# Feed-forward up products as three float32r products of split slots and split weights

## What is computed

```python
def ff(w1e, w2e, w3e):
    h = jax.nn.gelu(xf @ w2e * (xf @ w1e), approximate=False)
    return h @ w3e
y_all = jax.vmap(ff)(w1, w2, w3)      # w1, w2: (8, 128, 256), w3: (8, 256, 128)
y = y_all[m, jnp.arange(n)]           # each token takes the output of one expert
```

## Time and profile before

| | us |
|---|---|
| median of 3 runs | 568.18 |
| lowest, highest run | 567.49, 568.57 |
| span of the profiled execution (8050 instructions) | 554.8 |
| PE busy | 475.4 (86%) |
| DVE busy | 368.3 (66%) |
| ACT busy | 230.6 (42%) |
| POOL busy | 160.9 (29%) |
| up products in the chain that ended last | 4% of the span |

### The profile page before, as it was taken

The page is one execution under the profiler, slowest core; times in us unless marked ns, Lnnn a source line. Parts: engine busy times, 40 slices in busy tenths (PEclk is TensorE's granted clock), DMA queues, the critical chain, the costliest instruction groups (busy, mean ns, idle before and its releaser), DMA issues.

```text
span 554.8 us, 8050 instructions
## 1 busy us (share of the span) xinstructions
PE 475.4 (86%) x2788; PEld 263.0 (47%) x2788; DVE 368.3 (66%) x1023; ACT 230.6 (42%) x418; POOL 160.9 (29%) x200
## 2 busy tenths in 40 slices
PE   3877877899999999998999899999979889888940
PEld 2434344454454545544563555355444536555630
DVE  3635888766767676677658675857883645765685
ACT  1262531643463355426432842364144142445432
POOL 4311222401313241224302430313233465052432
PEclk9989998999999999999999999999998899899985
DMA  7500000000030003000300030011043052023224
GB/s 208 175 2 2 2 1 2 1 1 2 2 79 2 0 4 79 1 2 4 77 2 2 3 77 2 2 47 33 1 155 76 25 159 100 2 63 95 63 67 99
DMA packets 19093, 23.82 MB, mean 43 GB/s; under 512 B 2630, under 2 KB 15374, under 8 KB 18158
## 3 DMA queue, kind: packets, MB, share of 16 engines
q1 hardware_dynamic: 15308, 18.19, 12.0%
q0 software_dynamic: 1648, 4.07, 2.7%
q10 hardware_dynamic: 2098, 1.05, 0.7%
HBM read 16.71 MB, written 6.28 MB: 41 GB/s over the span
## 4 chain that ended last, share of the span: by engine, by line
PE 69%; DVE 13%; ACT 9%; issue 4%; POOL 2%; DMA 1%; ACTq 1%; POOLq 0%; DVEq 0%
PE ps_r L990 8%; PE ps_r L1017 7%; PE ps_st L955 6%; PE ps_r L860 5%; PE ps_r L709 5%; PE ps_st L1235 4%; ACT pt L1895 4%; PE ps_st L944 4%; PE ps_r L1006 3%; PE ps_r L763 3%; PE ps_r L837 3%; DVE rmax_a L1333 2%; PE ps_st L744 2%; PE ps_st L747 2%; PE ps_r L969 2%
## 5 line engine op out<-in xcount | busy, mean ns | idle before, releaser
L600 POOL TENSOR_TENSOR qkr<-qkr,prod 128x512 f32<-128x512 f32 (+1 forms) x48 | 52.3, 1096 | 191.3 <-DVE prod L1459 190.3
L1333 DVE TENSOR_REDUCE rmax_a<-ps_r 128x2 f32<-128x512 f32 (+1 forms) x96 | 61.2, 686 | 32.5 <-PE ps_r L837 32.3
L1895 ACT ACTIVATE pt<-ps_st 128x1024 f32<-128x1024 f32 x48 | 46.6, 1025 | 61.3 <-PE ps_st L747 61.3
L1333 DVE TENSOR_REDUCE rmax<-ps_r 128x2 f32<-128x512 f32 (+1 forms) x96 | 60.7, 683 | 15.3 <-PE ps_r L969 15.0
L709 PE MATMUL ps_r<-cbt 128*128 128x256 bf16 (+1 forms) x192 | 62.0, 323 | 2.6 <-ACT qbuf L1932 1.0
L1904 ACT ACTIVATE pt<-ps_st 128x1024 f32<-128x1024 f32 x48 | 47.2, 1022 | 32.4 <-PE ps_st L955 32.4
L637 POOL TENSOR_TENSOR oT<-pvb,oT 128x1024 f32<-128x1024 f32 x14 | 32.8, 2369 | 78.9 <-DMA oT<-inv_dram 78.9
L990 PE MATMUL ps_r<-pt,vb 128*64 128x512 f32 x192 | 48.2, 607 | 4.5 <-ACT pt L1904 2.7
L1017 PE MATMUL ps_r<-wqkv,xT_b 128*128 128x512 f32 x96 | 45.6, 612 | 4.1 <-DVE rmax_a L1333 3.5
L709 PEld LDWEIGHTS ps_r<-cbt 128*128 128x128 bf16 x192 | 18.6, 97 | 46.5 <-issue 34.2
L955 PE MATMUL ps_st<-qbuf,kbuf 64*128 64x512 f32 x288 | 39.8, 408 | 0.0
(11 more groups left out here) (238 smaller groups left out, 883.2 us busy)
## 6 DMA issues: line engine op xcount, KB each, us to landing
oT<-inv_dram SPq DMA_DIRECT2D x14, 512.0 KB, 5.5
xs_dram<-pvb SPq DMA_DIRECT2D x1, 2048.0 KB
pt<-in_L_ffn_w SPq DMA_DIRECT2D x2, 1024.0 KB, 7.7
ys_dram<-qkr SPq DMA_DIRECT2D x14, 128.0 KB, 1.8
qkr<-xs_dram POOLq DMA_DIRECT2D x4, 256.0 KB, 4.1
x_all<-in_L_attn_x ACTq DMA_DIRECT2D x1, 896.0 KB, 6.2
pvb<-xs_dram POOLq DMA_DIRECT2D x3, 256.0 KB, 4.8
out<-x_all SPq DMA_DIRECT2D x1, 640.0 KB, 3.9
```

What stands on the lines that cost most here:

```text
L600: nc.gpsimd.tensor_tensor(part, part, prod[:, (3 * t + i) % 2, 0:w], ALU.add).then_inc(add_in, 1)
L1333: nc.vector.tensor_reduce(heads_of(i), ps_r[:, b, :].rearrange("p (h k) -> p h k", h=4 if i < 4 else 2), AX.X, ALU.max).then_inc(free[b], 1)
L1895: nc.scalar.activation(pt_a(kind)[:, 8 * half:8 * half + 8, :], ps_st[:, c % 2, :, :].rearrange("p b (h t) -> p (b h) t", h=4), ACT.Exp, s ...
```

## The change

Each fp32 up product becomes three float32r products that add up in PSUM: high slots times high weights, high slots times low weights, low slots times high weights. A high part is the value as a float32r tile holds it, written by an ACT copy; a low part is the value less its high part, by a DVE subtraction.

- Weights: in the last attention step ACT makes the high parts in four copies of 1024 elements a row (`high_weights`) into `qbuf[0]`, and DVE the low parts in four subtractions (`low_weights`) into `qbuf[1]`, which holds the queries of sequence 7 until their scores are done.
- Slots: `take_slots` writes the high part into `kbuf[0]`, and DVE's new `low_slots(n)` the low part, from the same PSUM bank. DVE now frees the bank; ACT tells of the high part by `xg_hi_in`.
- `up(n)` waits for `xg_hi_in`, issues the products with high slots of all its tiles, waits for `emptied(xg{n})`, and issues the products with low slots.

```diff
+        whi, wlo = (b[:, :] for b in qbuf)
...
-        xgT = [xT_a, xT_b]
+        xg_hi, xg_lo = (kbuf[0][:, 2 * T * i:2 * T * (i + 1)].rearrange("p (a t) -> p a t", a=2) for i in range(2))
...
+        whi_in, wlo_in, xg_hi_in = sem("whi_in"), sem("wlo_in"), sem("xg_hi_in")
...
             def up(n, i, g):
 
-                emptied(pe, NB, f"xg{n}")
+                pe.wait_ge(xg_hi_in, n + 1)
                 if n > 1:
                     pe.wait_ge(prod_e, n - 1)
                 for t, tile in enumerate(g):
-                    mm = nc.tensor.matmul(ps_st[:, n % 2, t, :], xgT[n % 2][:, P * t:P * (t + 1)],
-                                          w12_flat[:, bass.ds(expert[tile] * 2, 2 * HID)], start=True, stop=True)
+                    rows, at = xg_hi[:, n % 2, P * t:P * (t + 1)], bass.ds(expert[tile] * 2, 2 * HID)
+                    nc.tensor.matmul(ps_st[:, n % 2, t, :], rows, whi[:, at], start=True, stop=False)
+                    nc.tensor.matmul(ps_st[:, n % 2, t, :], rows, wlo[:, at], start=False, stop=False)
+                emptied(pe, NB, f"xg{n}")
+                for t, tile in enumerate(g):
+                    mm = nc.tensor.matmul(ps_st[:, n % 2, t, :], xg_lo[:, n % 2, P * t:P * (t + 1)],
+                                          whi[:, bass.ds(expert[tile] * 2, 2 * HID)], start=False, stop=True)
                 mm.then_inc(up_full, 1)
...
-            pe.wait_ge(w12_in, 32)
+            pe.wait_ge(whi_in, 4)
+            pe.wait_ge(wlo_in, 4)
...
                 if s == NB - 1:
+                    low_weights(s, 0)
+                    low_weights(s, 1)
+                    low_slots(0, GROUPS[0][1])
...
+            def low_weights(s, i):
+
+                dve.wait_ge(whi_in, 4)
+                dve.wait_ge(sc_b, E_B * s + (4, E_B)[i])
+                for k in range(2):
+                    to, hi = (x.rearrange("p (e w n) -> p e w n", e=E, w=2)[:, E // 2 * k:E // 2 * (k + 1), i]
+                              for x in (wlo, whi))
+                    TT(to, w12[:, E // 2 * k:E // 2 * (k + 1), i], hi.bitcast(F32), ALU.subtract).then_inc(wlo_in, 1)
+
+            def low_slots(n, g):
+
+                b, w = filled(dve, NB, f"xg{n}"), len(g) * P
+                dve.wait_ge(xg_hi_in, n + 1)
+                TT(xg_lo[:, n % 2, 0:w], ps_r[:, b, 0:w], xg_hi[:, n % 2, 0:w].bitcast(F32), ALU.subtract) \
+                    .then_inc(free[b], 1)
...
                     take_hidden(n - 1, GROUPS[n - 1][1])
+                if n + 1 < NG:
+                    low_slots(n + 1, GROUPS[n + 1][1])
                 if n > 1:
                     take_outputs(n - 2, GROUPS[n - 2][1])
...
+                    high_weights(0, 3)
                 take_weights(s, 0)
                 exp(s, 2)
                 exp(s, 3)
+                if s == NB - 1:
+                    high_weights(3, 4)
...
-                nc.scalar.activation(xgT[n % 2][:, 0:w], ps_r[:, b, 0:w], ACT.Copy).then_inc(free[b], 1)
+                nc.scalar.activation(xg_hi[:, n % 2, 0:w], ps_r[:, b, 0:w], ACT.Copy).then_inc(xg_hi_in, 1)
+
+            def high_weights(lo, hi):
+
+                act.wait_ge(w12_in, 32)
+                for k in range(lo, hi):
+                    cols = slice(2 * E * HID // 4 * k, 2 * E * HID // 4 * (k + 1))
+                    nc.scalar.activation(whi[:, cols], w12_flat[:, cols], ACT.Copy).then_inc(whi_in, 1)
```

## The result

The changed kernel took 576.27 us (median of 4 runs, 573.88 to 579.98), the kernel before beside it 568.38: ratio 1.013 (1.009 to 1.017), 7.9 us slower. Two later comparisons gave 1.016 (1.013 to 1.018) and 1.015 (1.013 to 1.017). The sign was as forecast, the size was not: 3.25 us were forecast, 8 to 9 came. The ratios leave out executions over 1.5% above the fastest of the same kernel and are not the quotients of the two medians, from which they differ by up to 0.3%.

The account below looks back on a forecast made before the run. PE was taken to bound the kernel, 69% of its chain of waits. Terms 1.55 + 3.6 - 2.0 - 0.25 + 0.35 gave +3.25 us on 568.18: 571.4 us, range 568.4 to 574.0.

Parts of the forecast that it names:

- groups 5, 9, 11, 13: Odd feed-forward groups: the table read waits for the low slots, 0.9 us for each of four, +3.6 us.
- groups 0 to 3 (start of up(4)): First feed-forward groups: low_slots(3) stands behind slots(1) on DVE, so up(4) starts at 492.05 instead of 490.51, +1.55 us.
- even groups 4, 6, 10, 12, 14: Feed-forward groups without a table read, low slots ready early: shorter products gain 0.40 us each, -2.0 us.
- groups 7 and 8: Feed-forward loop: ACT's two table loads cover PE's delay and group 8's gain; up(7) ends earlier, -0.25 us for both.
- group 15 to the end: Last, one-tile group: low part ready 0.9 us after its start, so it and the tail end 0.35 us later.
- preparation: Last attention step: ACT's four copies and DVE's four subtractions of weights fit idle time, cost 0.
- The held table read: Odd groups: PE's table read, behind the low products' open wait, starts about 0.95 us after the first product.
- The rule of the Trainium skill: PE's sequencer fetches on past an open wait; rival that the table read is not held: 566.7 us, 12%.
- TensorE falls to 1.2 GHz: Rival, group 3: its new wait drops the clock for 3.4 us, +0.6 to +1.5 us, 572.0 to 572.9; 18%.
- The 13.4 us outside the span: Whole kernel: the time between the 554.8 us profiled span and the 568.18 us median, taken as unchanged.
- The bound of 1.6 us: Preparation: were DVE's last two weight subtractions twice as slow, invert_weights would start up to 1.6 us late.
- My own sign of being wrong: Listed sign against the forecast: the last attention step takes longer than now; no size given.

Follow-up runs that it names:

- after_again: The changed kernel again, unchanged, for a closer time and a second profile, on the quick chip: 565.02 us beside 555.51 for the kernel before, ratio 1.016.
- fp32_late_free: The kernel before with fp32 products, plus the changed kernel's waits for an unused DVE difference ahead of the table read: 563.57 us beside 555.51, ratio 1.012.
- read_early: The changed kernel with the table read issued between the high products and the wait for the low slots: 578.61 us beside 569.07, ratio 1.018.
- before_again: The kernel before, unchanged, run again for a second profile: 569.25 us beside 569.07, ratio 1.000.
- low3_early: The changed kernel with low_slots(3) moved ahead of slots(1) on DVE: 574.31 us beside 568.78 for the kernel before, ratio 1.010.
- low_first_unchecked: The changed kernel with low_first's order and the table read's bounds check skipped: 568.51 us beside 568.78 for the kernel before, ratio 1.000.
- low_first_unchecked_2: The kernel of low_first_unchecked run again, on the quick chip: 555.85 us, ratio 0.997 to the kernel before.
- low_first: The changed kernel with every low_slots(n + 1) ahead of take_hidden(n - 1) on DVE: 572.72 us beside 568.78 for the kernel before, ratio 1.007.
- unchecked_after: The changed kernel with the bounds check of the table read's values skipped: 560.04 us, ratio 1.007 to the kernel before.

## Why the prediction came out as it did
Forecast and measured terms, the latter as changed (after_again) less before in the table of periods (the loop's terms and the end add up to +6.6):

| term | forecast | measured |
|---|---|---|
| groups 5, 9, 11, 13 | +3.6 | +3.63 |
| groups 0 to 3 (start of up(4)) | +1.55 | +2.49 (group 3 +3.04, groups 0 to 2 -0.55) |
| even groups 4, 6, 10, 12, 14 | -2.0 | -0.35 |
| groups 7 and 8 | -0.25 | +0.47 |
| group 15 to the end | +0.35 | +0.36 |
| preparation | 0, at most 1.6 | 0 on slow chips, 1.6 to 4.8 on the quick one |

- **The held table read** was right to 0.2 us: it starts 1.03 us behind the first product (forecast 0.95) in groups 5, 7 and 9, 1.06 to 1.13 in 11 and 13 (once, in group 5 of the first profile, 1.29), and fp32_late_free shows that a read that late costs this much with the old products. The rule of the Trainium skill that I weighed against it ("Perfetto Trace Analysis", Per-engine timelines: the sequencer goes on to the next instruction while a wait is open), taken alone, would have had these groups at before's length; the traces do not bear it out for a sequencer's own step. The forecast held read and checks for one block of 1.60 us and did not ask where else it could stand; read_early answers that.
- **Group 3** had the right mechanism: its low products started 3.43 us behind up(3), and the hidden values were turned 1.69 behind them (forecast 1.60). The forecast +1.55 is where up(4) starts and holds an end of up(2) 0.65 earlier; measured is +2.49, of which the lower clock in group 3 makes 1.3 (0.48 in the transposes, 0.85 in the down products), so 1.2 is left. The -0.55 of groups 0 to 2 is a matter of clock: in that profile of before group 1 ran at half clock and took 4.77, in before_again 3.89, as in after_again. Beside before_again, groups 0 to 2 are 0.3 longer, not shorter, and 2.1 is left for the 1.55. So the size is right to 0.5 us, at full clock and no better.
- **The lower clock**, the rival "TensorE falls to 1.2 GHz", came true on top of the forecast, and it went on into group 4, whose products took 2.88 instead of 1.64. It was priced at 0.6 to 1.5 and took about 2.5 in two groups; before's own half clock in group 1 cost that kernel 0.9. The cause I gave it, the new wait, is doubtful: low3_early, low_first_unchecked and low_first_unchecked_2 have no such wait and a drop 4.2 to 4.4 us behind up(3) all the same. Between up(0) and up(15) the twelve profiles with float32r products show 3.4 to 17.1 us at half clock, the eight with fp32 products 0 to 6.8. So a lower clock goes with this change, and no run here isolates why.
- **Even groups** gained 0.26 to 0.34, not 0.40: the float32r products start every 0.23 us (0.22 taken, 0.24 the other end) and the first of six later by 0.1. Group 4's half clock makes the other 1.25 of this term's error of 1.65 (-0.35 for the forecast -2.0), the largest within the loop.
- **Groups 7 and 8**: the forecast let ACT's table loads cover PE's delay. But on ACT take_slots(8) stands ahead of gelu(7), and gelu(7) ahead of the loads. The held read delays the turned slots, take_slots(8) waits until 506.59 in after_again, and the loads begin 4.40 us behind up(7) instead of 3.92 (504.23, up(7) at 500.31). That is the +0.47: I had left out who waits behind the waiting engine.
- **Group 15 to the end** came out at +0.36 for +0.35, but partly by luck: the stretch lasts 25.42 to 26.09 us in three fp32 profiles of the quick pace, none of which has a late low part, and 26.27 in low_first_unchecked_2, which has none either.
- **The 13.4 us outside the span** was the step that was simply false. Time is span plus 1.8. It did not change the difference, but it hid that the profile and the times were of two chips, on only one of which the preparation costs something.
- **The preparation** was costed by durations and idle time of DVE alone. The bound of 1.6 us held for twice the duration; one instruction took 5.2 to 8.3 us where 1.13 was forecast and 1.22 to 1.42 is its length alone. My own sign of being wrong, a last attention step longer than before, came on the quick chip.

Of the 8 to 9 us on the quick chip, then: about 6.6 in loop and tail by one pair of profiles, of which 1.7 net are the lower clock; the rest most likely in the preparation, whose blocked difference varies from execution to execution. On a slow chip, where no difference is blocked, 7.9 were measured; the first profiles of the kind have the loop at 66.9 against 59.8 us, 6.0 of the 7.1 outside groups 13 and 14, where both profiles have a further hole. How much of that is waits and how much a clock at 0.50 more often, stays open: there low_first lost 4 us to before with every wait gone but the checks, and its profile has 10.2 us of the loop at half clock against 0.7 in before_again.

The best version is not one with float32r products: the kernel before with its read unchecked, 0.995 and 0.994, is faster than both.

## What to carry to other kernels
Before a product is shortened, ask what was running in its shadow: here a sequencer's table read of 2.2 us lay under products of 1.7 us, and a change that saves 0.3 us in every second group while it puts one wait ahead of that read loses 0.9 in the others. Putting the wait behind the sequencer's steps gained 0.2 to 0.3 us a group and nothing in the whole (read_early), closing it before it is reached 3.5 to 5 us (low_first), shortening the steps 5.0 (unchecked_after). And work put into an engine's idle time may not be free where another engine can block it.

## What the hardware showed
- A bounds check costs PE's sequencer 0.29 us for each value read, 1.15 us for four values, more than any of the reads took (0.33 to 1.01).
- A table read whose own semaphore had long come started only with the weight load ahead of it, when that load's wait closed: 1.02 to 1.13 us behind the first product in groups 5 to 13 of the quick chip's profiles of the changed kernel, against 0.00 to 0.17 in before.
- A DVE subtraction of two SBUF operands that takes 1.22 us alone took 5.2 to 8.3 us beside a row of GpSimd products.
- The same program ran about 2% quicker on one chip than on three others. On the slower ones the profiles show a stretch of some 4 to 7 us between 441 and 453 us in which PE finishes nothing or next to nothing, and then its clock at 1.2 GHz for up to 10 us; the profiles of the quick pace do not have it. Why a chip does that stays open.
